# Routing of a fused AdaLN, RG-LRU and top-2 MoE block: logits from x2, ranking on logits, half 1's second norm and modulation on ScalarE

## What is computed

```
h = layernorm(x) * (1 + ca) + sa
x = x + ga * attn(h)            # RG-LRU mixer and gated MLP; the result is called x2 here
h = layernorm(x) * (1 + cb) + sb
logits = h @ gate_w             # 8 experts
p = softmax(logits); the two largest p are kept and divided by their sum
x = x + gb * (sum over the chosen e of p_e * (gelu(h @ w1[e] + b1[e]) @ w2[e] + b2[e]) + h)
```

## Time and profile before

| | us |
|---|---|
| three timed runs | 319.52, 322.95, 323.54; median 322.95 |
| profiled execution | 318.49 |
| its span, first to last instruction | 316.7 |
| TensorE busy | 273.1 (86%) |
| VectorE busy | 194.7 (61%) |
| ScalarE busy | 180.4 (57%) |
| GpSimd busy | 114.9 (36%) |

### The profile page before, as it was taken

The page is one execution under the profiler, slowest core; times in us unless marked ns, Lnnn a source line. Parts: engine busy times, 40 slices in busy tenths (PEclk is TensorE's granted clock), DMA queues, the critical chain, the costliest instruction groups (busy, mean ns, idle before and its releaser), DMA issues.

```text
span 316.7 us, 4350 instructions
## 1 busy us (share of the span) xinstructions
PE 273.1 (86%) x1556; PEld 229.6 (72%) x1556; DVE 194.7 (61%) x450; ACT 180.4 (57%) x290; POOL 114.9 (36%) x97
## 2 busy tenths in 40 slices
PE   0799999958998999686959779999999999999780
PEld 0685446347686888565736669999999999999780
DVE  4766719739645276266495576767676767675520
ACT  5166589762497039251423669494949494949000
POOL 6000000000225033307227530656565656565651
PEclk9999999976999999996656999999999999999997
DMA  7960000000007564602104596393939393917231
GB/s 233 387 185 0 2 1 0 0 0 2 0 0 252 170 161 71 201 0 86 52 19 132 178 274 193 104 288 109 284 111 283 112 283 103 248 17 200 19 45 25
DMA packets 32726, 38.25 MB, mean 121 GB/s; under 512 B 7989, under 2 KB 28333, under 8 KB 32685
## 3 DMA queue, kind: packets, MB, share of 16 engines
q1 hardware_dynamic: 26816, 29.90, 30.0%
q0 software_dynamic: 4928, 7.44, 10.6%
q10 hardware_dynamic: 956, 0.59, 0.6%
HBM read 31.96 MB, written 8.90 MB: 129 GB/s over the span
## 4 chain that ended last, share of the span: by engine, by line
PE 70%; DVE 9%; ACT 8%; issue 6%; DMA 3%; POOL 2%; POOLq 0%; SPq 0%; ACTq 0%; DVEq 0%
PE bank L842 16%; PE bank L864 15%; PE bank L549 14%; PE bank L608 8%; PE bank L560 3%; DMA a_col<-in_L_attn_a_param 2%; PE bank L828 2%; PE bank L568 2%; PE bank L859 2%; PE bank L858 2%; PE bank L541 1%; DVE u L1303 1%; POOL v_lo L1652 1%; PE bank L699 1%; PE bank L753 1%
## 5 line engine op out<-in xcount | busy, mean ns | idle before, releaser
L1704 POOL DMA_INDIRECT out_x<-y_tok,meta x24 | 51.6, 2149 | 50.8 <-DVE y_tok L1576 44.6
L864 PE MATMUL bank<-w_hi,own 128*128 128x256 f32 x256 | 48.0, 286 | 1.8 <-DVE y_tok L1576 1.8
L842 PE MATMUL bank<-xe_hi,w_hi 128*128 128x320 f32 x128 | 39.7, 310 | 3.4 <-DVE xe_lo L1554 3.4
L864 PEld LDWEIGHTS bank<-w_hi,own 128*128 128x128 f32 x256 | 40.4, 191 | 2.4 <-issue 2.0
L1558 DVE TENSOR_TENSOR own<-own_raw,own 128x256 fp32r<-128x256 f32 x64 | 27.2, 425 | 23.5 <-ACT own L1134 18.9
L842 PE MATMUL bank<-xe_lo,w_hi 128*128 128x320 f32 x128 | 39.6, 309 | 0.0
L842 PE MATMUL bank<-xe_hi,w_lo 128*128 128x320 f32 x128 | 39.6, 309 | 0.0
L1128 ACT ACTIVATE own_raw<-bank,b1c 128x320 f32<-128x320 f32 x64 | 33.8, 529 | 8.5 <-PE bank L842 8.4
L864 PE MATMUL bank<-w_lo,own 128*128 128x256 f32 x128 | 36.2, 283 | 0.0
L1134 ACT ACTIVATE own<-own_raw 128x320 fp32r<-128x320 f32 x64 | 28.7, 461 | 0.0
L1695 POOL DMA_INDIRECT gb_rows<-gb_table,meta x24 | 24.4, 1016 | 9.4 <-issue 7.0
(11 more groups left out here) (211 smaller groups left out, 614.2 us busy)
## 6 DMA issues: line engine op xcount, KB each, us to landing
e_raw<-in_L_ffn_w SPq DMA_DIRECT2D x16, 1024.0 KB
x_rows<-in_L_attn_x SPq DMA_DIRECT2D x1, 2560.0 KB
xe_tok<-x_rows SPq DMA_DIRECT2D x8, 256.0 KB
raw_m<-in_L_attn_up_W SPq DMA_DIRECT2D x2, 768.0 KB, 9.7
x_tok<-in_L_attn_x SPq DMA_DIRECT2D x2, 512.0 KB, 5.1
out_x<-x_tok SPq DMA_DIRECT2D x1, 1024.0 KB
wmod<-in_L_wmod SPq DMA_DIRECT2D x1, 768.0 KB, 12.1
raw_m<-in_L_attn_down_W SPq DMA_DIRECT2D x1, 768.0 KB, 13.4
```

The lines of the kernel that those rows point to most:

```text
L842: ins = nc.tensor.matmul(bank[b][:, 0:CAP], l, r, start=(c == 0 and t == 0), stop=(c == KD - 1 and t == 2))
L864: ins = nc.tensor.matmul(bank[b][0:n, 0:D], l, r, start=(c == 0 and t == 0), stop=(c == KE - 1 and t == 2))
L1704: nc.gpsimd.indirect_dma_start(out_rows, bass.IndirectOffsetOnAxis(ap=ids[0:n, e, k, E:E + 1], axis=0), y_tok[e % 2][0:n, k, :], None, com ...
```

## The change

Logits: VectorE multiplies gate_w by 1 + cb and by sb for each batch (gate_by_batch, shift_by_batch) early on, and TensorE sums both over the features (gate_sums, all partitions alike). `x2_and_logits` makes, for each dt as soon as its x2 is there, the transposes and the products of x2 with gate_by_batch. `token_logits` then takes mean times sum off, multiplies by the inverse deviation and adds the shift's sum; no normed or modulated value is needed for it. `choose` ranks these logits themselves, ahead of `centre` and the exp; `weights` holds what follows the exp.

Half 1's norm goes to ScalarE (`norm2`, with scale rstd and bias centred, which is minus mean times rstd); the modulation of both halves goes there too (`modulate2`). numerators(0) comes behind keep_h2(0) and w2_hi_of(0); numerators(1) comes ahead of keep_h2(1). VectorE makes x2_of(1) in two parts with slots(0) and weights(0) between them. The fillers are 11, 4 and 30 where they were 6 and 16. A last ScalarE instruction of the routing is a Gelu on a small tile.

```
--- before.py
+++ after.py
@@ -109,6 +109,7 @@
...
+    order.take("gate_sums")
 
...
     take_up(1, 3)
     take_up(1, 4)
     take_up(1, 5)
     take_xh2(0)
     order.take(("down", 1, 0))
-    order.take(("logits", 0), drains=2)
     take_h2t(0)
+    order.take(("places", 0))
     order.take(("down", 1, 1))
-    order.take(("places", 0))
+    take_x2t(1)
+    order.take(("logits", 1))
     order.take(("cwT", 0))
-    take_x2t(1)
+    order.take(("busy", 1), drains=0, bank=3)
+    order.take(("xh2", 1, 0), drains=2, bank=3)
+    order.take(("xh2", 1, 1), drains=2)
+    order.take(("places", 1))
+    order.take(("busy", 3), drains=0, bank=1)
+    order.next = 6
+    order.take(("h2t", 1, 0))
+    order.take(("h2t", 1, 1), bank=1)
     take_biases(0)
-    order.take(("busy", 1), drains=0)
-    take_xh2(1)
-    order.take(("logits", 1), drains=2)
-    take_h2t(1)
-    order.take(("places", 1))
     order.take(("cwT", 1))
     take_biases(1)
     order.take(("busy", 2), drains=0)
...
+        gate_by_batch, shift_by_batch = [rt[:, n].rearrange("p t e -> p (t e)").rearrange("p (k b e) -> p k b e", k=KD, b=B) for n in (4, 8)]
+        gate_sums = new("gate_sums", [2, B, E])
+        centred = new("centred", [TH])
...
+            pe.wait_ge(gates_scaled, 2)
+            b, ps = begin("gate_sums")
+            for g, w in enumerate((gate_by_batch, shift_by_batch)):
+                for dt in range(KD):
+                    ins = nc.tensor.matmul(ps[:, g * B * E:(g + 1) * B * E], ones.to_broadcast([P, P]), w[:, dt].rearrange("p b e -> p (b e)"),
+                                           start=(g == 0 and dt == 0), stop=(g == 1 and dt == KD - 1))
+            end(ins, b)
...
-            def x2_to_tokens(hf):
-                pe.wait_ge(x2_done, KD * (hf + 1))
-                to_tokens("x2t", hf, xT)
+            def x2_and_logits(hf, dt):
+
+                pe.wait_ge(x2_done, KD * hf + dt + 1)
+                for p in range(2):
+                    b, ps = begin(("x2t", hf, p)) if dt == 0 else (order.at[("x2t", hf, p)][0], bank[order.at[("x2t", hf, p)][0]])
+                    for q in range(2):
+                        t = hf * TH + 2 * p + q
+                        ins = nc.tensor.transpose(ps[:, q * D + dt * P:q * D + (dt + 1) * P], xT[:, dt, t * P:(t + 1) * P], ident[:])
+                    if dt == KD - 1:
+                        end(ins, b)
+                b, ps = begin(("logits", hf)) if dt == 0 else (order.at[("logits", hf)][0], bank[order.at[("logits", hf)][0]])
+                for j in range(TH):
+                    t = hf * TH + j
+                    ins = nc.tensor.matmul(ps[:, j * E:(j + 1) * E], xT[:, dt, t * P:(t + 1) * P], gate_by_batch[:, dt, t * P // S, :],
+                                           start=(dt == 0 and j == 0), stop=(dt == KD - 1 and j == TH - 1))
+                if dt == KD - 1:
+                    end(ins, b)
...
-            def logits(hf):
-                b, ps = begin(("logits", hf))
+            def h2_to_tokens(hf):
                 for dt in range(KD):
...
-                end(ins, b)
+                to_tokens("h2t", hf, hT)
...
             def turn_weights(hf):
-                pe.wait_ge(top_done, 2 * hf + 2)
+                pe.wait_ge(top_done, 3 * hf + 3)
...
-            x2_to_tokens(0)
+            for dt in range(KD):
+                x2_and_logits(0, dt)
             up(1, 3)
             up(1, 4)
             up(1, 5)
             xhat2_blocks(0)
             down(1, [0])
-            logits(0)
-            to_tokens("h2t", 0, hT)
+            h2_to_tokens(0)
+            places(0)
             down(1, [1])
-            places(0)
+            x2_and_logits(1, 0)
             turn_weights(0)
-            x2_to_tokens(1)
+            x2_and_logits(1, 1)
+            pe.wait_ge(w1_hi_done, 1)
+            stay_busy(("busy", 1), w1_hi[0].rearrange("p k n -> p (k n)"), 11)
+            xhat2_blocks(1)
+            places(1)
+            stay_busy(("busy", 3), w1_hi[0].rearrange("p k n -> p (k n)"), 4)
+            h2_to_tokens(1)
             second_biases(0)
-            pe.wait_ge(w1_hi_done, 1)
-            stay_busy(("busy", 1), w1_hi[0].rearrange("p k n -> p (k n)"), 6)
-            xhat2_blocks(1)
-            logits(1)
-            to_tokens("h2t", 1, hT)
-            places(1)
             turn_weights(1)
             second_biases(1)
-            stay_busy(("busy", 2), w1_hi[0].rearrange("p k n -> p (k n)"), 16)
+            stay_busy(("busy", 2), w1_hi[0].rearrange("p k n -> p (k n)"), 30)
...
+            def modulate2(hf):
+
+                for dt in range(KD):
+                    b, ps = full(("xh2", hf, dt))
+                    for q in range(BH):
+                        bb = hf * BH + q
+                        nc.scalar.activation(hT[:, dt, bb * S:(bb + 1) * S], ps[:, q * S:(q + 1) * S], ACT.Identity,
+                                             scale=M(CB, dt, bb), bias=M(SB, dt, bb)).then_inc(drained[b], 1)
+
+            def norm2(hf):
+
+                act.wait_ge(centred_done, 1)
+                for j in range(TH):
+                    b, ps = full(("x2t", hf, j // 2))
+                    ins = nc.scalar.activation(xhat2[:, j, :], ps[:, j % 2 * D:(j % 2 + 1) * D], ACT.Identity,
+                                               scale=rstd[:, hf * TH + j:hf * TH + j + 1], bias=centred[:, j:j + 1])
+                    if j % 2:
+                        ins.then_inc(drained[b], 1)
+                for p in range(2):
+                    until_drained(("x2t", hf, p))
+                act.sem_inc(xhat_done, 1)
...
             def numerators(hf):
                 ts = slice(hf * TH, (hf + 1) * TH)
-                until_drained(("logits", hf), 2)
+                act.wait_ge(top_done, 3 * hf + 1)
                 nc.scalar.activation(rt[:, 1, ts, :], rt[:, 0, ts, :], ACT.Exp).then_inc(exp_done, 1)
...
             v_hi_of(NH * KF - 1)
+            modulate2(0)
+            keep_h2(0)
+            w2_hi_of(0)
             numerators(0)
-            keep_h2(0)
-
-            w2_hi_of(0)
             keep_weights(0)
             ln_root(4)
-            keep_biases(0)
-            keep_x2(1)
+            norm2(1)
+            modulate2(1)
             numerators(1)
             keep_h2(1)
+            keep_x2(1)
+            keep_biases(0)
             keep_weights(1)
             keep_biases(1)
             w1_hi_of(1)
+            nc.scalar.activation(centred[:], centred[:], ACT.Gelu).then_inc(gelu_ready, 1)
...
-            st.mark(nc.vector.tensor_scalar(mod[:, 2 * CB:2 * CB + 2, :], mod[:, 2 * CB:2 * CB + 2, :], 1.0, None, ALU.add))
+            st.link(nc.vector.tensor_scalar(mod[:, 2 * CB:2 * CB + 2, :], mod[:, 2 * CB:2 * CB + 2, :], 1.0, None, ALU.add))
+            dve.wait_ge(ffn_in, 16 * 3)
+            gates_now = gate_w[:].rearrange("p k (o e) -> p k o e", o=1).to_broadcast([P, KD, B, E])
+            for w, which in ((gate_by_batch, CB), (shift_by_batch, SB)):
+                by_batch = mod[:, 2 * which:2 * which + 2, :].rearrange("p k (b o) -> p k b o", o=1).to_broadcast([P, KD, B, E])
+                nc.vector.tensor_tensor(w, gates_now, by_batch, ALU.mult).then_inc(gates_scaled, 1)
...
-            def centre(hf):
+            def token_logits(hf):
 
                 ts = slice(hf * TH, (hf + 1) * TH)
+                bs = slice(hf * BH, (hf + 1) * BH)
+
...
+                lg = rt[:, 0, ts, :].rearrange("p (b q) e -> p b q e", b=BH)
                 b, ps = full(("logits", hf))
-                lg = ps[:, 0:TH * E].rearrange("p (t e) -> p t e", e=E)
-                nc.vector.tensor_reduce(big[:, ts], lg, mybir.AxisListType.X, ALU.max).then_inc(drained[b], 1)
+                dve.wait_ge(mv_done, hf + 3)
+                st.link(nc.vector.tensor_tensor(lg, per_token(mv[:, ts, 0]), per_batch(0), ALU.mult))
+                nc.vector.tensor_tensor(lg, ps[:, 0:TH * E].rearrange("p (b q e) -> p b q e", b=BH, e=E), lg, ALU.subtract).then_inc(drained[b], 1)
                 until_drained(("logits", hf))
-                nc.vector.tensor_tensor(rt[:, 0, ts, :], lg, across(big[:, ts]), ALU.subtract).then_inc(drained[b], 1)
+                if hf:
+                    inverse(hf)
+                    nc.vector.scalar_tensor_tensor(out=centred[:], in0=mv[:, ts, 0], scalar=-1.0, in1=rstd[:, ts],
+                                                   op0=ALU.mult, op1=ALU.mult).then_inc(centred_done, 1)
+                st.link(nc.vector.tensor_tensor(lg, lg, per_token(rstd[:, ts]), ALU.mult))
+                st.link(nc.vector.tensor_tensor(lg, lg, per_batch(1), ALU.add))
+
+            def inverse(hf):
+                ts = slice(hf * TH, (hf + 1) * TH)
+                dve.wait_ge(std_done, hf + 3)
+                st.link(nc.vector.reciprocal(rstd[:, ts], std[:, ts]))
...
             def choose(hf):
 
                 ts = slice(hf * TH, (hf + 1) * TH)
-                dve.wait_ge(exp_done, hf + 1)
-                pe_ = rt[:, 1, ts, :]
```

(38 more changed lines are left out.)

15 lines of the change are left out of this document (8 added, 7 removed).

## The result

The changed kernel has a median of 318.24 us in 20 runs (314.06 to 322.79), the kernel before 323.08 us in 20 runs beside them (317.5 to 325.73). The ratio is 0.990 (95% interval 0.986 to 0.994): about 1% faster, less than the 2% that would count as faster. The medians are those of all 20 runs, the ratio leaves out each kernel's slow ones. Forecast were 317.4 us and a gain of 5.6 us; by the medians the gain is 4.8, by the ratio 3.2. The time is 0.8 us from the forecast; of the gain between half and nine tenths is there, and not by the forecast steps.

What follows compares the result with a forecast made beforehand. It took half 1's routing as a chain of short steps with no engine full. The chain alone gave 8.6 us, the later-ending fillers left 5.6; from the timed median 322.95 that made 317.4 us, range 312.5 to 321.5.

Steps and rivals of the forecast that it cites:

- The routing: Down(1, 1)'s end to half 1's first scatter: ranking leaves the path, exp and row copies set it; scatter at 154.6.
- Late next is the filler: Ahead of turn(0): 30 fillers take 9.4 us and end at 169.05, 3.2 us after the rows arrive.
- Ahead of the routing: Up to down(1, 1)'s end: down(1, 0) starts at 131.45, down(1, 1) ends at 140.85, 0.36 us later than before.
- token_logits(0), four steps of 0.2: VectorE ahead of v_of(10): four logit steps lie inside the 0.2 us already taken, as v_of(10) waits for ScalarE anyway.
- The wait for the bank of x2t(0, 0): TensorE at up2(1, 5): the bank is free only after keep_x2(0), costing 0.2 us (0 to 1).
- Down(1, 0) "needs 4.2 us": TensorE's product down(1, 0) ahead of the routing: it takes 4.2 us, as from 129.56 to 133.76 before.
- B: Rival: the clock falls already at 145 and is low in the whole routing; gain 0.1, 322.9 us; chance 0.12.
- The early VectorE work: Before recur(0): two products and one wait on small tiles cost 0 to 0.5 us, taken at 0.
- The 141.9 us behind it: From turn(0) to the end: the experts' part moves along unchanged at 141.9 us.
- A: Rival: the clock never falls behind 157 us, the rows set the end; gain 8.6, 314.4 us; chance 0.25.
- C: Rival: clock low in the whole routing and all 30 fillers; turn(0) 3.9 us later, 326.9 us; chance 0.08.
- D: Rival: each table switch holds ScalarE as long again as its load, 1.28; gain 3.0, 320.0 us; chance 0.05.

Runs made afterwards that it cites:

- after: The changed kernel as it is, its first profiled execution, against the kernel before: 318.43 us profiled; timed median 318.24 us, ratio 0.990.
- again: The changed kernel itself with no further edit, timed and profiled a second time against the kernel before: 317.1 us, ratio 0.994.
- fillers16: The changed kernel with 16 last fillers in place of 30: 311.84 us, ratio 0.976 to the kernel before.
- no_early_gelu: The changed kernel without its last small Gelu on ScalarE: 314.65 us, ratio 0.989 to the kernel before.
- half1_on_vector: The changed kernel with norm and modulation of half 1 back on VectorE: 320.03 us, ratio 0.999 to the kernel before.
- logits0_late: The changed kernel with token_logits(0) moved behind v_of(11), the last v, on VectorE: 315.95 us, ratio 0.988 to the kernel before.

## Why the prediction came out, step by step

**The routing: right.** From the end of down(1, 1) to the first scatter 13.75 us were forecast in place of 23.1; seven profiles of versions with this order have 14.0 (the profile of after, with the stall, 16.1). Norm2 and modulate2 took 1.94 and 1.93 (taken: 1.9). The exp and what hangs on it set the scatter, not the ranking: in the second profile the row copies and weights(1) both end by 158.1, the scatter starts at 158.88, and slot_b was there at 155.6. Putting half 1's norm and modulation back on VectorE costs 2.3 us of it.

**Late next is the filler: right.** The rows are there 11.3 behind the first scatter (taken: 11.25), the second bias and the fillers end later: 30 fillers took 8.8 to 9.9 us (taken: 9.4), and with 16 TensorE waits for the rows again. From down(1, 1) to turn(0) 28.35 was forecast; the unchanged kernel's second profile has 27.74.

**Ahead of the routing: wrong.** Down(1, 1) was to end at 140.85. It ended at 145.46 and 144.88, and at 142.09 and 141.82 in two variants whose order there is the same. From down(0, 0) to down(1, 0) all seven profiles with the changed order there took 29.54 to 29.58 us, where 26.39 is the old kernel's and 28.29 was forecast: 3.2 us lost in place of 1.9. The rest of the 4.0 to 4.6 is the clock and what lies ahead of down(0, 0). Term by term:
- "token_logits(0), four steps of 0.2, stands ahead of v_of(10), which waits for ScalarE anyway: it is inside the 0.2." It is not inside. One of the four steps took 1.03 beside GpSimd's v_lo, both v_more start behind them (at 128.66), choose(0) slows the last v_lo, and TensorE's wait before down(1, 0) went from 2.59 to 3.27. Moving the four steps behind the last v gave 1.0 us back.
- The wait for the bank of x2t(0, 0): "I take 0.2 (0 to 1)". The prediction's own times, 126.9 and 126.3, give 0.6. Its row shows 0.48, and the first product behind it starts 0.86 behind the one ahead of it where the step is 0.23: 0.63 lost.
- Down(1, 0) "needs 4.2 us". That is its price at 2.4 GHz. Of the seven profiles in which the wait ahead of it is 3.22 to 3.27, five have the clock at 1.2 GHz for part of it, and it then took 5.56 (again) to 7.01 (fillers16). In no_early_gelu and half1_on_vector the clock stayed and it took 4.19. None of the five profiles with token_logits(0) late has the fall. So the fall is not certain, and it costs 1.4 to 2.8 us when it comes. None of the rivals had it: B put the fall at 145, behind the down products.
- The early VectorE work "taken at 0": in the profile of after down(0, 0) is 0.59 late. It is not shown to be a price of this work: the twelve profiles of the changed kernel and its variants, all with this work, have down(0, 0) at 102.52 to 104.74, the old kernel at 103.17 and 103.35. A half-clock stretch near 70 us in each profile, and one near 50 us in most, of different lengths, lie ahead of it.
- "The 141.9 us behind it move along unchanged." In after they did (141.8). In nine of the other eleven profiles of changed kernels they are 142.9 to 143.2, with a half-clock stretch of 3 to 4.5 us in the first layer of expert 0 or 1. The old kernel's second profile has two such stretches, so that the change brings them is not shown; a sum that takes the clock there as full leaves out 1.1 us and more.

The forecast 1.70 for the moved logits themselves held (the gelu is 2.32 late: 1.7 and the 0.59), and the bank wait is within its bounds of 0 to 1.

**How it still came out.** Losses of 4.0 to 4.6 us ahead of the routing should have left 1 to 1.6 us of the 5.6; turn(0) of the second profile, 172.62, is 2.2 earlier than before, with 0.6 from the end of down(1, 1) to turn(0), which took 27.74. Of profile against profile nothing (after) or 1.2 us (again) is left of the span. By the medians the gain is 4.8 and 2.7. Executions in which down(1, 0) keeps its clock can stand beside the others (as in no_early_gelu, turn(0) 5.0 us earlier), and the old kernel's own executions spread upward from its first profile (317.5 to 325.7); how much each of these gives is not shown. The forecast also took its base, 322.95, from three runs; beside the experiments the old kernel had medians of 319.5 to 319.9. That a sum over one profiled execution came within a microsecond of the median was luck.

**The rivals.** A: the changed kernel's executions with the highest mean clock, 0.961, took 314.1 to 315.1 us, which is about A's 314.4; but A's reason, that the clock stays up behind 157 us, is not shown, as none of them was profiled, and logits0_late, profiled with the same mean clock of 0.961, has it low from 157.5 to 164.3. B and C: the clock was not low through the whole routing in any profile of the changed kernel. D: no drain ahead of half 1's exp; it starts 0.02 behind its load (156.24 + 1.28 to 157.54), and the rule of the Trainium skill, page "ScalarE: Activation LUTs", section "What ACT_TABLE_LOAD costs", is not borne out at these two places. The early table was costless, as forecast.

## What to carry to other kernels

Work moved ahead of the product that everyone waits for costs more than its own time: it lengthens the wait of TensorE behind it, and that wait can cost the clock for the product itself. Put such work into a wait that is there already (logits(0) behind xhat2_blocks(0) was worth 3.4 us by the medians and 2.15 in the traces, on top of the logits' vector steps behind the last v; both together took the whole delay of down(1, 0) away). Fillers must end when the data lands: here 30 ended 2.4 us too late, with 8 the first expert ran at half clock in the one profile, and 16 had the lowest median of the three that were tried. And small VectorE steps with both inputs in SBUF are priced beside what GpSimd does at the time, not by their own row elsewhere.
